# Delta-rule attention with experts on one core: state updates as full 128-row products, and exponentials written in place

## The chip, the cores and the metric

One Trainium2 chip; the program runs on one of its cores. The metric is the device time of one execution in microseconds. TensorE makes the matrix products and transposes, VectorE, ScalarE and GpSimd (POOL in the profile) the elementwise work, SyncE (SP) issues most of the DMAs. SBUF is the on-chip memory of 128 partitions, PSUM the banks that TensorE writes to.

## The reference

A layer on x of 2 batches x 2048 tokens x 256. Attention has 16 heads of 128, in segments of 64 tokens, and carries a state per batch and head from segment to segment:

```python
def step(carry, seg):                       # one segment of 64 tokens
    mem, z = carry                          # [b, h, 128, 128], [b, h, 128, 1]
    qq, kk, vv = seg
    sigma_q = jax.nn.elu(qq) + 1.0
    att_dot = softmax(causal(qq @ kk.T / scale)) @ vv
    att_mem = sigma_q @ mem / (sigma_q @ z)
    sigma_k = jax.nn.elu(kk) + 1.0
    delta = vv - sigma_k @ mem / (sigma_k @ z)
    mem_new = mem + sigma_k.T @ delta
    z_new = z + sigma_k.sum(rows)
    att = beta * att_mem + (1.0 - beta) * att_dot
    ...
x = x + attention(layernorm(x))
x = x + experts(layernorm(x))               # router, 32 experts, a shared one
```

The feature map elu(a) + 1 is max(a, 0) + min(exp(a), 1).

## The kernel before

Two functions run one after the other: `attention` and `experts`. The change is in the first.

`attention` goes through 16 blocks (`NBLK`) of 128 tokens, that is two segments for each of the two batches, and in every block through 8 groups (`NG`) of two heads (`HG`): 128 groups, counted by `n`. The state of all heads stays in SBUF in `mem`, 129 columns per head and batch (`ZC`: 128 of `mem` and one of z). Each engine has its own hand-ordered queue; semaphores join them, and every engine executes strictly in its written order.

In one group TensorE does, in this order (`body` of the tensor block, L997 to L1046): the numerators of segment 0 (`numerators`, L883: features times state, for keys into PSUM bank `chain_k` and for queries into `chain_q`); after a wait for `ksig_ready`, the key projection of the next group (`project_t`, L838, 12 products of 128x128 by 256 columns); the transposes of the group before (L927); the state update of segment 0 (`update`, L899); the query projection of the next group; in group 6 the transposes of the next block's input; in group 0 half of the output projection (`project_out`, L945); the numerators of segment 1; the transposes of the probabilities (L936); the value projection (`project_v`, L850); in groups 3, 4 and 7 some small work for the block before (`x1_transposes`, `logits`, `pick_transposes`); the key transposes of the next group (`key_transposes`, L873); the update of segment 1; the products of probabilities and values (`attend`, L910, in the 64x64 form); and the scores of the next group (`scores`, L860).

An update computes the transposed key features times `dl`, in which partitions 0 to 63 hold the 64 tokens of batch 0 and partitions 64 to 127 those of batch 1. It makes four products, for each of two heads one of batch 0 into `chain_k` (rows 0 to 63 of the array) and one of batch 1 into `chain_q` (rows 64 to 127), each with 129 moving columns. The stationary operand is `ksig`, the transposed key features. A product on f32 operands is two matmul instructions in the trace, each with its weight load; a transpose is one. The form in the profile, as 64*128 or 128*128, is the part of the array that an instruction uses.

The features come about in four steps per group: ScalarE copies the projection (`qraw`, `kraw`) and writes its exponential to `ex_q` and `ex_k` (`queries` L385, `keys` L392); GpSimd caps it at 1 in place (`cap_queries` L305, `cap_keys` L311); VectorE adds the larger of the projection and 0 and writes `sigq` and `sigk` (`sigma_q` L564, `sigma_k` L572), which have two buffers, by the parity of the group. TensorE transposes `sigk` into `bank_k`, and ScalarE copies that to `ksig` (`key_rows`, L408), once the update of segment 1 of the group before has read the old `ksig`.

VectorE makes `dl` (`delta`, L579), subtracts the update from the state (`state`, L597; `mem_ready` lets the next numerators go), and does the softmax sums, the layer norms and the router's choice of experts. ScalarE also reads out the memory's answer (`read_out`, L415) and copies values (`values`, L401); `attend` waits for the latter.

Of the kernel before, what the change touches and what calls it, by code (L numbers as in the profile page):

```python
# [19 lines left out]
HG = 2  # L20
# [45 lines left out]
def attention(nc, ctx, io, scratch):  # L66
# [31 lines left out]
    kraw = sb("kraw", [128, HG, 2, B, SEG])  # L98
    ex_q = sb("ex_q", [128, HG * 2 * B * SEG])
    ex_k = sb("ex_k", [128, HG * 2 * B * SEG])  # L100
    val = sb("val", [128, 2, HG, DK])
    vb = sb("vb", [128, 2, HG, DK])
    vo = sb("vo", [128, 2, HG, DK])
    ksig = sb("ksig", [128, HG, 2, DK])
    sm = sb("sm", [128, T, SEG])
# [172 lines left out]
    def _(pool):  # L278
# [17 lines left out]
        for half in range(2):  # L296
# [6 lines left out]
                       allow_small_or_imprecise_dtypes=True).then_inc(s["desc_ready"], 1)  # L303

        def cap_queries(n):  # L305
            pool.wait_ge(s["q_exp"], n + 1)
            stand_alone(pool, s["pool_noted"])
            nc.gpsimd.tensor_scalar(ex_q[:, :], ex_q[:, :], 1.0, None, ALU.min  # L308
                                    ).then_inc(s["q_min"], 1)

        def cap_keys(n):  # L311
            pool.wait_ge(s["k_exp"], n + 1)
            stand_alone(pool, s["pool_noted"])
            nc.gpsimd.tensor_scalar(ex_k[:, :], ex_k[:, :], 1.0, None, ALU.min  # L314
                                    ).then_inc(s["k_min"], 1)
# [52 lines left out]
    def _(act):  # L368
# [16 lines left out]
        def queries(n, first_ever=False):  # L385
            act.wait_ge(s["q_mm"], n + 1)
            nc.scalar.activation(flat(qraw), bank_q[:, :], ACT.Copy).then_inc(s["q_raw"], 1)  # L387
            if not first_ever:
                act.wait_ge(s["q_sig"], n)
            nc.scalar.activation(ex_q[:, :], bank_q[:, :], ACT.Exp).then_inc(s["q_exp"], 1)  # L390

        def keys(n, first_ever=False):  # L392
            act.wait_ge(s["k_mm"], n + 1)
            if not first_ever:
                act.wait_ge(s["s_mm"], n)
            nc.scalar.activation(flat(kraw), bank_k[:, :], ACT.Copy).then_inc(s["k_raw"], 1)
            if not first_ever:
                act.wait_ge(s["k_sig"], n)
            nc.scalar.activation(ex_k[:, :], bank_k[:, :], ACT.Exp).then_inc(s["k_exp"], 1)  # L399

# [7 lines left out]
        def key_rows(n, first_ever=False):  # L408
            act.wait_ge(s["kt_mm"], n + 1)
            if not first_ever:  # L410
                act.wait_ge(s["upd_mm"], 2 * n)
            nc.scalar.activation(ksig[:, :, :, :].rearrange("p j s d -> p (j s d)"), bank_k[:, :],  # L412
                                 ACT.Copy).then_inc(s["ksig_ready"], 1)

# [33 lines left out]
        queries(0, True)  # L448
        values(0, True)
        key_rows(0, True)  # L450

# [52 lines left out]
    def _(dve):  # L504
# [59 lines left out]
        def sigma_q(n, par):  # L564
# [3 lines left out]
                out=sigq[:, par, :, :, :, :].rearrange("p j s b t -> p (j s b t)"),  # L568
                in0=bank_q[:, :], scalar=0.0, in1=ex_q[:, :], op0=ALU.max, op1=ALU.add
                ).then_inc(s["q_sig"], 1)  # L570

        def sigma_k(n, par):  # L572
            dve.wait_ge(s["k_min"], n + 1)
            nc.vector.scalar_tensor_tensor(
                out=sigk[:, par, :, :, :, :].rearrange("p j s b t -> p (j s b t)"),
                in0=bank_k[:, :], scalar=0.0, in1=ex_k[:, :], op0=ALU.max, op1=ALU.add
                ).then_inc(s["k_sig"], 1)
# [150 lines left out]
        for seg in range(2):  # L728
            nc.vector.memset(dl[seg][:, :, DK:ZC], -1.0)
        nc.vector.memset(gsx[:, :, :], SENT)  # L730
        nc.vector.memset(glist[:, :, :], SENT)
# [95 lines left out]
    def _(pe):  # L827
# [71 lines left out]
        def update(n, seg):  # L899
# [3 lines left out]
            for j in range(HG):  # L903
                for b in range(B):
                    ins = mm((chain_k, chain_q)[b][:, j * ZC:(j + 1) * ZC],  # L905
                             ksig[ROWS[b], j, seg, :], dl[seg][ROWS[b], j, :],
                             start=True, stop=True)
# [754 lines left out]
```

## Time and profile before

| | |
|---|---|
| median of 3 runs | 1832.46 us (1832.45 to 1833.88) |
| the profiled execution, its own time | 1832.18 us |
| its span, first to last instruction | 1830.4 us |
| mean granted TensorE clock | 0.985 |
| TensorE busy: matmul | 1732.8 us, 95% of the span |
| TensorE busy: weight load, beside it | 1475.5 us, 81% |
| VectorE busy | 1206.7 us, 66% |
| ScalarE busy | 803.0 us, 44% |
| GpSimd busy | 913.0 us, 50% |
| update products (L905), 2 x 1024 instructions | 297 ns mean of one |
| key-row copies (L412), 128 | 598 ns mean of one |

How to read it: a matmul's duration in the profile runs to the modelled end of its result, so neighbours overlap; what an instruction costs in a dense stretch is the distance from its start to the next one's. The engine on which nearly no idle time is left sets the time, and a wait of another engine costs nothing by itself. Names such as bank_k<-ident,sigk give what is written and what is read; xN is the number of instructions merged in a row.

### The profile page before, as it was taken

What the parts mean: (1) busy time and instruction counts of PE and PEld (TensorE: products, weight loads), DVE (VectorE), ACT (ScalarE), POOL (GpSimd) and SP (SyncE); (2) the same over time, 40 slices, a digit from 0 to 9 for tenths busy, and PEclk for the clock granted to TensorE, in tenths of its full rate; (3) what the DMA queues carried; (4) which work ended last, traced back from release to release, by engine and by line L of the source; (5) the groups of instructions that cost most, each with busy time, mean ns of one, the idle gap of its engine ahead of it and who ended that gap; (6) DMA issues with size and microseconds to landing.
All of it is one profiled execution on the core that took longest, in us unless ns stands there. A gap on an engine that the chain in (4) does not pass through costs nothing. (4 is left out here: it accounts for less than half of the span.)

```text
span 1830.4 us, 45891 instructions
## 1 busy us (share of the span) xinstructions
PE 1732.8 (95%) x17990; PEld 1475.5 (81%) x17990; DVE 1206.7 (66%) x3996; ACT 803.0 (44%) x1934; POOL 913.0 (50%) x826
## 2 busy tenths in 40 slices
PE   6999999999999999999999999999999999984988
PEld 5788888888888888888888888888888888862545
DVE  6756757576767667575767676675757675756544
ACT  3544545353535455453535354554535353521131
POOL 4655646454646555464546465554645464620261
PEclk9999999999999999999999999999999999997999
DMA  4200000001000000000010000000000100006956
GB/s 152 81 10 25 15 19 15 25 8 32 8 14 25 15 25 15 19 15 25 7 32 7 15 25 15 25 15 20 17 22 8 32 8 9 25 14 203 273 136 196
DMA packets 83431, 75.24 MB, mean 41 GB/s; under 512 B 20992, under 2 KB 74128, under 8 KB 82960
## 3 DMA queue, kind: packets, MB, share of 16 engines
q1 hardware_dynamic: 78992, 65.96, 11.9%
q0 software_dynamic: 3376, 5.55, 1.5%
q8 instruction: 144, 2.36, 0.6%
q10 hardware_dynamic: 848, 0.79, 0.2%
q14 instruction: 71, 0.58, 0.1%
HBM read 47.78 MB, written 24.47 MB: 39 GB/s over the span
## 5 line engine op out<-in xcount | busy, mean ns | idle before, releaser
L323 POOL TENSOR_TENSOR vb<-val,beta_rows 128x512 f32<-128x512 f32 x128 | 169.3, 1322 | 243.8 <-ACT val L405 243.8
L419 ACT ACTIVATE am<-chain_q,rdq 128x128 f32<-128x128 f32 x512 | 159.3, 365 | 274.2 <-DVE rdq L585 274.0
L601 DVE TENSOR_TENSOR mem<-mem,chain_k 128x258 f32<-128x258 f32 x256 | 107.7, 421 | 252.0 <-PE chain_q L905 252.0
L348 POOL TENSOR_TENSOR sm<-sm,smx 128x256 f32<-128x256 f32 x128 | 78.5, 613 | 313.7 <-DVE smx L757 313.7
L951 PE MATMUL bank_o<-wo,att 128*128 128x256 f32 x1024 | 228.1, 381 | 0.9 <-ACT att L433 0.9
L951 PEld LDWEIGHTS bank_o<-wo,att 128*128 128x128 f32 x1024 | 193.6, 191 | 26.7 <-issue 1.3
L314 POOL TENSOR_SCALAR ex_k<-ex_k 128x512 f32<-128x512 f32 x128 | 191.0, 1492 | 43.9 <-ACT ex_k L399 43.9
L308 POOL TENSOR_SCALAR ex_q<-ex_q 128x512 f32<-128x512 f32 x128 | 190.1, 1485 | 0.3 <-POOL vo L332 0.3
L895 PE MATMUL chain_k<-mem,sigk 128*64 128x129 f32 x2048 | 165.5, 281 | 20.9 <-DVE mem L601 20.9
L905 PE MATMUL chain_k<-dl,ksig 64*128 64x129 f32 x1024 | 181.4, 297 | 2.2 <-ACT am L419 1.6
L905 PE MATMUL chain_q<-dl,ksig 64*128 64x129 f32 x1024 | 181.6, 297 | 0.0
L905 PEld LDWEIGHTS chain_k<-dl,ksig 64*128 64x128 f32 x1024 | 132.4, 186 | 45.3 <-issue 42.3
L332 POOL TENSOR_TENSOR vo<-val,vb 128x512 f32<-128x512 f32 x128 | 164.3, 1284 | 0.0
L591 DVE SCALAR_TENSOR_TENSOR dl<-chain_k,rdk,vb 128x128 f32<-128x128 f32 x512 | 154.6, 343 | 6.2 <-DVE rdk L582 0.8
L895 PE MATMUL chain_q<-mem,sigq 128*64 128x129 f32 x2048 | 157.7, 273 | 0.0
L355 POOL TENSOR_TENSOR pd<-sm,sinv 128x256 f32<-128x256 f32 x128 | 78.4, 612 | 153.0 <-DVE sinv L765 153.0
L412 ACT ACTIVATE ksig<-bank_k 128x512 f32<-128x512 f32 x128 | 76.6, 598 | 160.3 <-PE chain_q L905 155.6
L895 PEld LDWEIGHTS chain_k<-mem,sigk 128*64 128x64 f32 x2048 | 108.9, 137 | 43.9 <-issue 29.8
L387 ACT ACTIVATE qraw<-bank_q 128x512 f32<-128x512 f32 x128 | 76.4, 597 | 135.2 <-PE bank_q L846 135.2
L905 PEld LDWEIGHTS chain_q<-dl,ksig 64*128 64x128 f32 x1024 | 132.5, 186 | 0.0
L895 PEld LDWEIGHTS chain_q<-mem,sigq 128*64 128x64 f32 x2048 | 122.3, 136 | 0.0
L846 PE MATMUL bank_k<-xt_hi,w_hi 128*128 128x256 f32 x512 | 117.1, 311 | 1.1 <-DVE xt_lo L559 1.1
(193 smaller groups left out, 4337.1 us busy)
## 6 DMA issues: line engine op xcount, KB each, us to landing
w<-in_L_ffn_w_dram SPq DMA_DIRECT2D x16, 512.0 KB, 8.1
expert_rows<-w_in SPq DMA_DIRECT2D x16, 288.0 KB, 2.2
expert_sums<-zero SPq DMA_DIRECT2D x16, 272.0 KB, 5.0
x_in<-in_L_attn_x_dram SPq DMA_DIRECT2D x16, 256.0 KB, 3.0
x_res<-in_L_attn_x_dram SPq DMA_DIRECT2D x16, 256.0 KB, 3.2
x_rows<-w_in SPq DMA_DIRECT2D x16, 256.0 KB, 2.0
x_normed_t<-x1t SPq DMA_DIRECT2D x16, 256.0 KB, 2.1
xt_all<-x_normed_t SPq DMA_DIRECT2D x4, 1024.0 KB, 13.3
```

What stands on the lines that cost most here:

```text
L308: nc.gpsimd.tensor_scalar(ex_q[:, :], ex_q[:, :], 1.0, None, ALU.min).then_inc(s["q_min"], 1)
L314: nc.gpsimd.tensor_scalar(ex_k[:, :], ex_k[:, :], 1.0, None, ALU.min).then_inc(s["k_min"], 1)
L323: nc.gpsimd.tensor_tensor(vb[:, :, :, :].rearrange("p s j d -> p s (j d)"), val[:, :, :, :].rearrange("p s j d -> p s (j d)"), rows.unsque ...
L332: nc.gpsimd.tensor_tensor(vo[:, :, :, :], val[:, :, :, :], vb[:, :, :, :], ALU.subtract).then_inc(s["vo_ready"], 1)
L348: nc.gpsimd.tensor_tensor(sm[:, :, :], sm[:, :, :], smx[:, :].unsqueeze(2).to_broadcast([128, T, SEG]), ALU.subtract).then_inc(s["s_shifte ...
L419: ins = nc.scalar.activation(am[:, par, seg, j, :], chain_q[:, j * ZC:j * ZC + DK], ACT.Copy, scale=rdq[:, seg, j:j + 1])
L591: ins = nc.vector.scalar_tensor_tensor(out=dl[seg][:, j, 0:DK], in0=chain_k[:, j * ZC:j * ZC + DK], scalar=rdk[:, seg, j:j + 1], in1=vb[:, ...
L601: ins = nc.vector.tensor_tensor(m, m, (chain_k, chain_q)[b][:, 0:HG * ZC].rearrange("p (j z) -> p j z", j=HG), ALU.subtract)
L846: ins = mm(out, w[:, g, m, c, col], x[:, c, :, :].rearrange("p s t -> p (s t)"), start=i == 0, stop=i == len(parts) - 1)
L895: ins = mm(out[ROWS[half], j * ZC:(j + 1) * ZC], sig[:, j, seg, b, :], mem[:, HG * g + j, b, :], start=True, stop=True)
L905: ins = mm((chain_k, chain_q)[b][:, j * ZC:(j + 1) * ZC], ksig[ROWS[b], j, seg, :], dl[seg][ROWS[b], j, :], start=True, stop=True)
L951: ins = mm(bank_o[:, b * D:(b + 1) * D], att[:, b * PIECES + i, :], wo[:, i, :], start=(i == 0 and b == 0), stop=(i == PIECES - 1), skip_g ...
```

## The change

- The copy of the transposed key features goes to `ksig` with one more dimension, the batch. Batch 0's 64 rows go to its own part of the buffer, batch 1's to another, and the other batch's rows of each part are zero, written once at the start by a memset on VectorE. The copy is so two instructions of 64 partitions instead of one of 128.
- The four products of an update take all 128 rows of `ksig` and of `dl`. The zero rows add nothing, so the results are the same.
- The exponentials are written to `sigq` and `sigk` themselves, capped there and turned into the features there; `ex_q` and `ex_k` go, and with them ScalarE's waits for `q_sig` and `k_sig`.
- ScalarE waits for `zero_ready` once before the first copy of key rows.

```diff
--- before.py
+++ after.py
@@ -96,12 +96,11 @@
     sigk = sb("sigk", [128, 2, HG, 2, B, SEG])
     qraw = sb("qraw", [128, HG, 2, B, SEG])
     kraw = sb("kraw", [128, HG, 2, B, SEG])
-    ex_q = sb("ex_q", [128, HG * 2 * B * SEG])
-    ex_k = sb("ex_k", [128, HG * 2 * B * SEG])
     val = sb("val", [128, 2, HG, DK])
     vb = sb("vb", [128, 2, HG, DK])
     vo = sb("vo", [128, 2, HG, DK])
-    ksig = sb("ksig", [128, HG, 2, DK])
+
+    ksig = sb("ksig", [128, HG, 2, B, DK])
     sm = sb("sm", [128, T, SEG])
     pd = sb("pd", [128, T, SEG])
     smx = sb("smx", [128, T])
@@ -302,16 +301,20 @@
         nc.gpsimd.iota(desc[:, :, :], pattern=[[-S, B], [-1, BLK]], base=N, channel_multiplier=0,
                        allow_small_or_imprecise_dtypes=True).then_inc(s["desc_ready"], 1)
 
+        def flat(t, n):
+
+            return t[:, n % 2, :, :, :, :].rearrange("p j s b t -> p (j s b t)")
+
         def cap_queries(n):
             pool.wait_ge(s["q_exp"], n + 1)
             stand_alone(pool, s["pool_noted"])
-            nc.gpsimd.tensor_scalar(ex_q[:, :], ex_q[:, :], 1.0, None, ALU.min
+            nc.gpsimd.tensor_scalar(flat(sigq, n), flat(sigq, n), 1.0, None, ALU.min
                                     ).then_inc(s["q_min"], 1)
 
         def cap_keys(n):
             pool.wait_ge(s["k_exp"], n + 1)
             stand_alone(pool, s["pool_noted"])
-            nc.gpsimd.tensor_scalar(ex_k[:, :], ex_k[:, :], 1.0, None, ALU.min
+            nc.gpsimd.tensor_scalar(flat(sigk, n), flat(sigk, n), 1.0, None, ALU.min
                                     ).then_inc(s["k_min"], 1)
 
         def values_kept(n, g, first_ever=False):
@@ -385,18 +388,14 @@
         def queries(n, first_ever=False):
             act.wait_ge(s["q_mm"], n + 1)
             nc.scalar.activation(flat(qraw), bank_q[:, :], ACT.Copy).then_inc(s["q_raw"], 1)
-            if not first_ever:
-                act.wait_ge(s["q_sig"], n)
-            nc.scalar.activation(ex_q[:, :], bank_q[:, :], ACT.Exp).then_inc(s["q_exp"], 1)
+            nc.scalar.activation(flat(sigq[:, n % 2]), bank_q[:, :], ACT.Exp).then_inc(s["q_exp"], 1)
 
         def keys(n, first_ever=False):
             act.wait_ge(s["k_mm"], n + 1)
             if not first_ever:
                 act.wait_ge(s["s_mm"], n)
             nc.scalar.activation(flat(kraw), bank_k[:, :], ACT.Copy).then_inc(s["k_raw"], 1)
-            if not first_ever:
-                act.wait_ge(s["k_sig"], n)
-            nc.scalar.activation(ex_k[:, :], bank_k[:, :], ACT.Exp).then_inc(s["k_exp"], 1)
+            nc.scalar.activation(flat(sigk[:, n % 2]), bank_k[:, :], ACT.Exp).then_inc(s["k_exp"], 1)
 
         def values(n, first_ever=False):
             act.wait_ge(s["v_mm"], n + 1)
@@ -409,8 +408,11 @@
             act.wait_ge(s["kt_mm"], n + 1)
             if not first_ever:
                 act.wait_ge(s["upd_mm"], 2 * n)
-            nc.scalar.activation(ksig[:, :, :, :].rearrange("p j s d -> p (j s d)"), bank_k[:, :],
-                                 ACT.Copy).then_inc(s["ksig_ready"], 1)
+            for b in range(B):
+                ins = nc.scalar.activation(
+                    ksig[ROWS[b], :, :, b, :].rearrange("p j s d -> p (j s) d"),
+                    bank_k[ROWS[b], :].rearrange("p (c d) -> p c d", d=DK), ACT.Copy)
+            ins.then_inc(s["ksig_ready"], 1)
 
         def read_out(n, par, seg):
 
@@ -447,6 +449,7 @@
         keys(0, True)
         queries(0, True)
         values(0, True)
+        act.wait_ge(s["zero_ready"], 2)
         key_rows(0, True)
 
         def body(blk, first, last):
@@ -566,14 +569,14 @@
             dve.wait_ge(s["q_min"], n + 1)
             nc.vector.scalar_tensor_tensor(
                 out=sigq[:, par, :, :, :, :].rearrange("p j s b t -> p (j s b t)"),
-                in0=bank_q[:, :], scalar=0.0, in1=ex_q[:, :], op0=ALU.max, op1=ALU.add
+                in0=bank_q[:, :], scalar=0.0, in1=sigq[:, par, :, :, :, :].rearrange("p j s b t -> p (j s b t)"), op0=ALU.max, op1=ALU.add
                 ).then_inc(s["q_sig"], 1)
 
         def sigma_k(n, par):
             dve.wait_ge(s["k_min"], n + 1)
             nc.vector.scalar_tensor_tensor(
                 out=sigk[:, par, :, :, :, :].rearrange("p j s b t -> p (j s b t)"),
-                in0=bank_k[:, :], scalar=0.0, in1=ex_k[:, :], op0=ALU.max, op1=ALU.add
+                in0=bank_k[:, :], scalar=0.0, in1=sigk[:, par, :, :, :, :].rearrange("p j s b t -> p (j s b t)"), op0=ALU.max, op1=ALU.add
                 ).then_inc(s["k_sig"], 1)
 
         def delta(n, seg):
@@ -727,6 +730,7 @@
         nc.vector.memset(mem[:, :, :, DK:ZC], 1.0 / DK)
         for seg in range(2):
             nc.vector.memset(dl[seg][:, :, DK:ZC], -1.0)
+        nc.vector.memset(ksig[:, :, :, :, :], 0.0)
         nc.vector.memset(gsx[:, :, :], SENT)
         nc.vector.memset(glist[:, :, :], SENT)
         nc.vector.memset(tmpx[:, :, :], SENT)
@@ -903,7 +907,7 @@
             for j in range(HG):
                 for b in range(B):
                     ins = mm((chain_k, chain_q)[b][:, j * ZC:(j + 1) * ZC],
-                             ksig[ROWS[b], j, seg, :], dl[seg][ROWS[b], j, :],
+                             ksig[:, j, seg, b, :], dl[seg][:, j, :],
                              start=True, stop=True)
             ins.then_inc(s["upd_mm"], 1)
```

## Rows read from the trace of the kernel before

**Rows 1.** the page's part 2, granted clock of TensorE in 40 slices, in tenths

```profile
PEclk9999999999999999999999999999999999997999
```

**Rows 2.** busy us (x instructions) of each engine in one steady block

```profile
320.96:421.53 100.57, 98.91 (x1091) 86.95 (x1091) 69.37 (x237) 47.44 (x115) 53.58 (x48) 1.00 0.06 18
```

**Rows 3.** waits of TensorE in ten steady blocks: total us, times, longest

```profile
PE chain_k L895 <- DVE mem L601: 10.8, 10, 1.1
PE bank_a L922 <- ACT val L405: 5.9, 20, 0.3
```

**Rows 4.** the same view, first block

```profile
PE bank_a L922 <- ACT val L405: 3.8, 6, 1.1
PE chain_k L895 <- DVE mem L601: 3.6, 6, 0.7
```

**Rows 5.** timeline of TensorE around update 0: start us, us, instructions

```profile
1004.26 0.40 PE L846 MATMUL bank_k<-xt_hi,w_lo 128*128 128x256 f32 x2
1004.50 0.60 PE L932 MATMUL bank_a<-by_piece,am 128*128 128x128 f32 x4
1005.03 0.37 PE L905 MATMUL chain_k<-dl,ksig 64*128 64x129 f32 x1
1005.03 0.37 PE L905 MATMUL chain_q<-dl,ksig 64*128 64x129 f32 x1
1005.24 0.27 PE L905 MATMUL chain_k<-dl,ksig 64*128 64x129 f32 x1
...
1005.36 0.27 PE L905 MATMUL chain_k<-dl,ksig 64*128 64x129 f32 x1
...
1005.67 0.51 PE L846 MATMUL bank_q<-xt_hi,w_hi 128*128 128x256 f32 x2
1006.02 0.40 PE L846 MATMUL bank_q<-xt_lo,w_hi 128*128 128x256 f32 x2
```

**Rows 6.** the same view, transposes that follow one another

```profile
977.33 0.60 PE L961 MATMUL bank_o<-ident,w_in 128*128 128x128 f32 x4
977.76 0.60 PE L878 MATMUL bank_k<-ident,sigk 128*128 128x128 f32 x4
```

**Rows 7.** the same view, output projection, and router products

```profile
1030.20 7.07 PE L951 MATMUL bank_o<-wo,att 128*128 128x256 f32 x32
1037.20 0.66 PE L895 MATMUL chain_k<-mem,sigk 128*64 128x129 f32 x8
...
988.50 0.97 PE L969 MATMUL bank_o<-gwt,x1t 128*128 128x32 f32 x8
989.31 0.63 PE L878 MATMUL bank_k<-ident,sigk 128*128 128x128 f32 x4
```

**Rows 8.** timeline of all engines around update 1

```profile
999.70 0.60 PE L878 MATMUL bank_k<-ident,sigk 128*128 128x128 f32 x4
...
1000.87 0.33 PE L922 MATMUL bank_a<-vo,pt 64*64 64x128 f32 x2
...
1001.05 0.60 ACT L412 ACTIVATE ksig<-bank_k 128x512 f32<-128x512 f32 x1 [0.56 <-PE chain_q L905]
...
1001.33 0.42 DVE L601 TENSOR_TENSOR mem<-mem,chain_q 128x258 f32<-128x258 f32 x1
...
1001.47 0.69 PE L869 MATMUL bank_s<-kraw,qraw 128*64 128x64 f32 x16
...
1001.98 0.61 PE L895 MATMUL chain_k<-mem,sigk 128*64 128x129 f32 x8
...
1002.97 0.51 PE L846 MATMUL bank_k<-xt_hi,w_hi 128*128 128x256 f32 x2
```

**Rows 9.** ScalarE by lines, a steady block: busy us, mean ns, idle before

```profile
L390 ACT ACTIVATE ex_q<-bank_q 128x512 f32<-128x512 f32 x8 | 4.7, 592 | 0.0
```

**Rows 10.** timeline of VectorE at the start

```profile
12.35 3.47 DVE L726 MEMSET mem<- 128x4096 f32 x1 [0.80 <-issue]
...
18.65 1.76 DVE L507 TENSOR_TENSOR w_lo<-w_in,w_hi 128x1536 fp32r<-128x1536 f32 x1 [2.62 <-ACT w_hi L374]
```

## The prediction

> **What bounds the kernel now.** I read the page's clock row first, then the busy times by stretch, then the waits of TensorE alone, and last the timeline of single product groups. The granted clock is nine tenths or more in 39 of the 40 slices [rows 1] and 1.00, the level of 2.4 GHz, in a steady block [rows 2], so between the two versions only instructions and waits can differ. The attention part, 128 groups of two heads in 16 blocks of 8, fills most of the span: a steady block takes 100.57 us, and 16 of them would be 1609 us of 1830. In it TensorE is busy 98.91 us, VectorE 69.37, ScalarE 47.44, GpSimd 53.58 [rows 2]. TensorE sets the pace, and its waits are few and regular: over ten blocks it waits 10 times for the state update on VectorE, 1.08 us each (after group 7 of a block), and 20 times for the copy of the values on ScalarE, 0.295 us each (groups 3 and 6) [rows 3]. The first block has more of both, 3.6 and 3.8 us over six or seven groups [rows 4]. So what one group's products cost on TensorE counts 128 times, save where one of these waits takes it up.
>
> **Part 1, the products.** Each update has four source products, each two instructions in the trace. Before, the product of batch 0 uses array rows 0 to 63 and that of batch 1 rows 64 to 127, and the rows show them as pairs: both start within 0.01 us, and the next pair 0.11 to 0.12 us later [rows 5]. So eight instructions take four steps. After, all eight use the full array and can only follow one another: eight steps.
>
> What this mode costs at its edges is to be seen too. The four transposes ahead of update 0 start at 1004.50 and the update at 1005.03, 0.53 us. Four transposes followed by others of the same kind take 0.43 us (977.33 to 977.76) [rows 6], so the switch into 64-row mode costs 0.10 us of drain. Its first pair is followed by the second only after 0.21 us (1005.03 to 1005.24), 0.10 more than a step: a weight load with nothing to hide it. From the last pair to the next work it is 0.20 us. Then the projection's first two products take 0.35 us (1005.67 to 1006.02), where two take 0.24 us elsewhere (1004.26 to 1004.50): again an uncovered load. Update 0 stands between two stretches of 128-row work, so after the change both switches go. Update 1 comes after 128-row transposes but ahead of 64x64 products, so only the switch into it goes.
>
> How fast a full-array f32 product with 129 moving columns repeats, no row shows. The nearest rows: 256 columns take 0.219 us each (32 in 7.00 us, 1030.20 to 1037.20, the last drain in it), so their weight load is hidden and half the columns would stream in 0.108 us; with 32 moving columns, where only the load of 128 columns can count, 8 take 0.81 us, 0.101 each (988.50 to 989.31) [rows 7]; the projections repeat at 0.119 us, with loads of the same size [rows 5]. I take 0.112 us: the stream of 129 columns (0.108, as in the pairs) and a few ns for the load, near the first row. The bounds are 0.101 and 0.119.
>
> Update 0, from the first transpose ahead of it to the third product of the projection: before 1006.02 - 1004.50 = 1.52 us. After 4 x 0.108 + 8 x 0.112 + 0.24 = 1.57 us. That is +0.05 us.
> Update 1, from the first key transpose to the first 64x64 product: before 1000.87 - 999.70 = 1.17 us [rows 8]. After 4 x 0.108 + 7 x 0.112 + 0.20 = 1.42 us. That is +0.25 us.
> Together +0.30 us a group; 128 groups make +38 us if no wait takes any of it.
>
> The Trainium skill speaks against this change more strongly: "TensorEngine Tiling (Array Packing)", section "Theoretical Speedup", gives up to a factor of two for a dimension of 64 or less. As a factor on the steps alone this would be 4 x 0.11 = 0.44 us more per update, 0.88 per group, +113 us in all, and a time of 1945. The trace has that factor on the steps but takes most of it back at the edges, which that section leaves out; I go by the rows.
>
> **What the waits take up.** In groups 3 and 6 TensorE waits 0.295 us for the values' copy, which ScalarE makes after another copy that itself follows work of TensorE ahead of update 1. The chain is released before update 1 and does not lengthen with it, so the 0.25 us of update 1 go into this wait. After group 7 the 1.08 us wait is for VectorE's chain of gate weights, picks, query features and state, released from the group's softmax early in the group; it takes both updates, 0.30 us. A steady block so grows by 8 x 0.30 - 2 x 0.25 - 0.30 = 1.6 us; 15 blocks 24 us. In the first block the waits of rows 4 (over 0.5 us each) take up update 1 in nearly every group, leaving 8 x 0.05 = 0.4 us. Sum +24.4 us.
>
> **Part 2, the key rows' copy.** One 128x512 copy of 0.60 us becomes two of 64 partitions with 512 elements each. No row shows the shorter form. Bounds: half each if partitions counted (nothing added), 0.60 each back to back (+0.60 us); I take the upper end less the 0.1 us by which neighbours overlap, since a copy's time goes with the elements per partition, +0.5 us per group. What is late next: the projection of keys waits for it. In the group shown the copy ends at 1001.65 and the projection starts at 1002.97, 1.32 us later, and TensorE shows no wait there [rows 8]. The +0.5 fits, and behind it on ScalarE only the memory read-out is queued, which needs the numerators that end after 1002.97. Cost nothing; without that cover, up to 0.5 x 128 = 64 us.
>
> **Part 3, exponentials in place.** Exponentials, caps and maxima keep count and size. Two waits of ScalarE go; the exponential of the queries already started with no idle time in front, 0.592 us each [rows 9], so nothing is gained. Cost nothing.
>
> **Part 4, the start.** The zeroing of the key-row buffer is a 128x1024 memset on VectorE. The 128x4096 one took 3.47 us, so about 0.87 us, in front of a 2.62 us idle time [rows 10]; ScalarE's new wait for it stands ahead of a copy that begins at 23.8 us, long after, and queues nothing. Cost nothing; uncovered, 0.9 us once.
>
> **The rivals.**
> *Weight loads are not hidden (slower by much).* If every full-array product paid load and stream, 0.21 us as the first after a switch does [rows 5]: update 0 is 4 x 0.108 + 8 x 0.21 + 0.24 - 1.52 = +0.83, update 1 0.43 + 7 x 0.21 + 0.20 - 1.17 = +0.93; 1.76 x 128 = 225 us, less the waits of 15 x 1.67 + 7.4 = 32: about +193, 2025 us. Against it: the 256-column products and the projections both hide a load of the same size [rows 5, 7]. Chance 0.03. The skill's "TensorE: Matmul & The Clock Gate", section "The mechanism" of its part on packing, says that weight loads overlap a running product only when the row group differs; that rule would give this case. The rows with full-array products disagree with it.
> *The waits move instead of shrinking (slower).* If the chains of ScalarE and VectorE start later with the update, nothing is taken up: +38, 1871 us. It could be so if they are not released where I read it. Chance 0.08.
> *The state update comes too late (slower).* Numerators start 1001.98, the state's last addition ends 1001.75 [rows 8]; the signal takes part of the 0.23 us. If the deeper products end 0.05 us later than the margin allows, 100 groups lose 5 us: 1862. It decides from about 0.1 us. Chance 0.05, inside the range.
> *The switches pay for the steps (faster).* Break-even: with a step of s us update 0 differs by 8s - 0.85 and update 1 by 7s - 0.54; a steady block has the first 7 times and the second 5 times uncovered, and their sum is zero at s = 0.095. Below it the kernel is faster. The densest products with small moving tiles, the scores, make 16 instructions in 0.51 us, 0.064 per pair [rows 8]; at that step updates differ by -0.34 and -0.09 us, times 128 about -55 us, 1778. Against it: nothing on the full array repeats in under 0.101 us, even with 32 columns [rows 7]. Chance 0.04. At the bound 0.101 itself a block grows by 0.6 us, +8 us, 1841: still slower.
> *The change does less than it says.* The longer step could be hidden wholly by waits: they amount to 1.67 us a block and stand in three groups of eight, so five groups must show it. Within 0.2%, by the same sum, only for a step of 0.092 to 0.098 us: chance 0.03.
> *The copies come late.* If two copies took over 1.9 us together (1.32 us slack): 0.02, from 0.3 us late about +38 more, 1895.
>
> **The numbers.** The profiled execution took 1832.18 us, the median of the runs 1832.46; +24.4 on the latter gives 1856.9. The likeliest case (step 0.108 to 0.119, waits taking up their part) has chance 0.75: at 0.108 a block grows by 1.2 us, 1850.5; at 0.119 by 2.2 us, 1866. The range 1844 to 1871 adds the late state update, half of the way to the 0.101 bound and the waits that move. About 0.2% (3.7 us) is what a measurement of this kernel can tell from no change. Faster 0.04, same 0.03, slower 0.93.
>
> **What would show it.** The timeline of the update: eight instructions of 128*128 form at 0.112 us steps, transposes ahead at 0.108 with no drain. Steady blocks of 102.2 us instead of 100.57. The value waits shrink from 0.295 to 0.05 us or go, the state wait from 1.08 to about 0.78. Key-row copies: two, 1.1 us from the first's start to the second's end, and TensorE without a wait ahead of the key projection. VectorE and GpSimd unchanged in busy time. Wrong would be a step outside 0.101 to 0.119, a new wait of TensorE for the key rows, or a wait for the state in every group.

## The result, and the profile after

The changed kernel takes 1857.93 us in the median, the kernel before 1832.64 us beside it: 1.0136 times as long, with a 95% interval of 1.0119 to 1.0153. The growth is 25.3 us; the forecast was 1857 us, 24.4 us more. One of the changed kernel's four executions took 6463.26 us at a mean granted clock of 0.418 and stays out of the ratio; the median of the other three is 1857.78 us, 25.1 us more. The profiled execution took 1858.08 us with a span of 1856.3 us.

The page of the changed kernel, its first part (busy us, share of the span, instructions):

```profile
PE 1772.1 (95%) x17990; PEld 1571.5 (85%) x17990; DVE 1218.3 (66%) x3997; ACT 876.8 (47%) x2062; POOL 917.5 (49%) x826
```

TensorE is busy 39 us longer than before, ScalarE 74 us (the second copy of the key rows), VectorE 12 us, GpSimd 5 us. Only TensorE is near its span.

One steady block, in the same view as [rows 2]:

```profile
325.24:427.46 102.22, 101.30 (x1090) 92.91 (x1091) 70.11 (x237) 52.02 (x123) 53.83 (x48) 1.00 0.06 18
```

The block takes 102.22 us where it took 100.57; the forecast was 102.2. The granted clock is 1.00 as before.

TensorE's waits in ten steady blocks (total us, times, longest), against [rows 3]:

```profile
PE chain_k L899 <- DVE mem L604: 8.3, 10, 0.8
```

The 20 waits for the value copies are gone from the view; what is left of them in the trace is 0.05 us each. The wait for the state after group 7 is 0.83 us instead of 1.08.

The timeline of TensorE around update 0, against [rows 5]; a row of L909 with x2 holds the two instructions of one product:

```profile
965.73 0.60 PE L936 MATMUL bank_a<-by_piece,am 128*128 128x128 f32 x4
966.17 0.39 PE L909 MATMUL chain_k<-dl,ksig 128*128 128x129 f32 x2
966.39 0.39 PE L909 MATMUL chain_q<-dl,ksig 128*128 128x129 f32 x2
966.62 0.39 PE L909 MATMUL chain_k<-dl,ksig 128*128 128x129 f32 x2
966.84 0.39 PE L909 MATMUL chain_q<-dl,ksig 128*128 128x129 f32 x2
966.98 0.48 PE L850 MATMUL bank_q<-xt_hi,w_hi 128*128 128x256 f32 x2
967.30 0.40 PE L850 MATMUL bank_q<-xt_lo,w_hi 128*128 128x256 f32 x2
```

Eight instructions of the update follow one another, two every 0.22 to 0.23 us; the last starts at 966.95 and the first of the projection at 966.98. From the first transpose to the third projection product it is 967.30 - 965.73 = 1.57 us (1.52 before). The four transposes now take 0.44 us, with no drain behind them, where they took 0.53.

The same view around update 1, against [rows 8]:

```profile
960.69 0.60 PE L882 MATMUL bank_k<-ident,sigk 128*128 128x128 f32 x4
961.13 0.39 PE L909 MATMUL chain_k<-dl,ksig 128*128 128x129 f32 x2
...
961.80 0.39 PE L909 MATMUL chain_q<-dl,ksig 128*128 128x129 f32 x2
962.12 0.33 PE L926 MATMUL bank_a<-vo,pt 64*64 64x128 f32 x2
```

962.12 - 960.69 = 1.43 us (1.17 before): eight steps take the place of four and only the entry is saved.

The costliest groups of the page that the change touches (busy us, mean ns | idle before, releaser):

```profile
L412 ACT ACTIVATE ksig<-bank_k 64x512 f32<-64x512 f32 x256 | 151.5, 592 | 192.1 <-PE chain_q L909 187.5
...
L909 PE MATMUL chain_k<-dl,ksig 128*128 128x129 f32 x1024 | 199.7, 276 | 2.4 <-ACT am L421 1.7
L909 PE MATMUL chain_q<-dl,ksig 128*128 128x129 f32 x1024 | 198.0, 275 | 0.0
```

### The profile page after: what moved, and what is told of

Read it like the earlier page. It is cut to its first block and busy times, and to the rows that moved or that the text cites. A ratio compares the mean times of both kernels' runs of the same rounds, so it can differ in the third digit from the quotient of the medians.

```text
span 1856.3 us, 46021 instructions
## 1 busy us (share of the span) xinstructions
PE 1772.1 (95%) x17990; PEld 1571.5 (85%) x17990; DVE 1218.3 (66%) x3997; ACT 876.8 (47%) x2062; POOL 917.5 (49%) x826
## 5 line engine op out<-in xcount | busy, mean ns | idle before, releaser
L604 DVE TENSOR_TENSOR mem<-mem,chain_k 128x258 f32<-128x258 f32 x256 | 107.9, 421 | 288.3 <-PE chain_q L909 287.2
L412 ACT ACTIVATE ksig<-bank_k 64x512 f32<-64x512 f32 x256 | 151.5, 592 | 192.1 <-PE chain_q L909 187.5
L317 POOL TENSOR_SCALAR sigk<-sigk 128x512 f32<-128x512 f32 x128 | 193.9, 1515 | 44.5 <-ACT sigk L398 44.5
L909 PE MATMUL chain_k<-dl,ksig 128*128 128x129 f32 x1024 | 199.7, 276 | 2.4 <-ACT am L421 1.7
L909 PE MATMUL chain_q<-dl,ksig 128*128 128x129 f32 x1024 | 198.0, 275 | 0.0
L311 POOL TENSOR_SCALAR sigq<-sigq 128x512 f32<-128x512 f32 x128 | 190.1, 1485 | 2.0 <-POOL vo L335 0.3
L899 PE MATMUL chain_k<-mem,sigk 128*64 128x129 f32 x2048 | 165.6, 281 | 17.2 <-DVE mem L604 17.2
L335 POOL TENSOR_TENSOR vo<-val,vb 128x512 f32<-128x512 f32 x128 | 164.1, 1282 | 0.0
L909 PEld LDWEIGHTS chain_k<-dl,ksig 128*128 128x128 f32 x1024 | 155.0, 191 | 4.9 <-DVE dl L594 3.2
L909 PEld LDWEIGHTS chain_q<-dl,ksig 128*128 128x128 f32 x1024 | 154.8, 191 | 0.0
L472 ACT ACTIVATE pt<-bank_s 128x256 f32<-128x256 f32 x128 | 49.3, 385 | 153.0 <-PE bank_s L944 153.0
```

The costliest lines, as they stand in the source:

```text
L311: nc.gpsimd.tensor_scalar(flat(sigq, n), flat(sigq, n), 1.0, None, ALU.min).then_inc(s["q_min"], 1)
L317: nc.gpsimd.tensor_scalar(flat(sigk, n), flat(sigk, n), 1.0, None, ALU.min).then_inc(s["k_min"], 1)
L335: nc.gpsimd.tensor_tensor(vo[:, :, :, :], val[:, :, :, :], vb[:, :, :, :], ALU.subtract).then_inc(s["vo_ready"], 1)
L412: ins = nc.scalar.activation(ksig[ROWS[b], :, :, b, :].rearrange("p j s d -> p (j s) d"), bank_k[ROWS[b], :].rearrange("p (c d) -> p c d", ...
L604: ins = nc.vector.tensor_tensor(m, m, (chain_k, chain_q)[b][:, 0:HG * ZC].rearrange("p (j z) -> p j z", j=HG), ALU.subtract)
L899: ins = mm(out[ROWS[half], j * ZC:(j + 1) * ZC], sig[:, j, seg, b, :], mem[:, HG * g + j, b, :], start=True, stop=True)
```

## Where the growth lies, group by group

The length of a group is taken from its first numerator product to that of the next group, worked out from the traces as the mean of 13 steady blocks. In these terms the changed kernel stands against the one before:

```
us            g0     g1     g2     g3     g4     g5     g6     g7    block
before      24.20  10.33  10.38  11.16  11.18  10.35  11.16  11.81  100.56
changed     24.50  10.62  10.63  11.17  11.48  10.78  11.24  11.85  102.26
difference   0.30   0.29   0.25   0.02   0.29   0.43   0.09   0.04    1.70
forecast     0.30   0.30   0.30   0.05   0.30   0.30   0.05   0.00    1.60
```

15 blocks of 1.70 us are 25.5 us, and the first block grew by 0.15 us. The stretch ahead of the first group changed by +0.6 us, that from the last group on by -0.3. So the growth is in the attention part, and its pattern is the forecast's, with one cell out of line: group 5.

## The experiments

Theory: TensorE sets the time; a full-array product repeats at 0.112 us, the mode switches that go give part back, and three waits a block take up part of the rest. The rivals: the second copy or the in-place exponentials carry part of it; the updates cost equal halves; the waits only move; the step is set by something else than the forecast took.

### Exponentials in place, alone

One of its two lines, against the kernel before:

```diff
-            nc.scalar.activation(ex_q[:, :], bank_q[:, :], ACT.Exp)
+            nc.scalar.activation(flat(sigq[:, n % 2]), bank_q[:, :], ACT.Exp)
```

> Only the exponentials in place; key rows copied in one piece and updates in the 64-row form, as before. Theory (serial products on TensorE make the whole growth): 1832.6 us, within 0.1% of before. Rival (the in-place writing or the two dropped waits of ScalarE shift work on ScalarE, VectorE and GpSimd so that TensorE waits more or less): a change of over 2 us either way.

Measured 1832.85 us against 1832.88 of before, ratio 0.9999 (0.9989 to 1.0008). A steady block is 100.54 us. This part of the change is free and brings nothing.

### Two key-row copies, with the updates in the 64-row form

```diff
-                             ksig[:, j, seg, b, :], dl[seg][:, j, :],
+                             ksig[ROWS[b], j, seg, b, :], dl[seg][ROWS[b], j, :],
```

> The changed kernel with the updates back in the 64-row form: two key-row copies of 64 partitions, the zeroed buffer and the exponentials in place stay. Theory: the copies fit into their slack of 1.32 us, so 1832.6 us, within 0.1% of before. Rival (the second copy carries part of the growth): 1835 to 1858 us, with a wait of TensorE ahead of the key projection.

Measured 1832.79 us, ratio 1.0000 (0.9991 to 1.0010). TensorE's waits in ten steady blocks are those of [rows 3]:

```profile
PE chain_k L899 <- DVE mem L604: 10.8, 10, 1.1
PE bank_a L926 <- ACT val L404: 6.0, 20, 0.4
```

None is for the key rows. The second copy, the zeroing and the new wait at the start cost nothing; all 25 us come from the form of the products.

### One update at a time

```diff
+                    rows = slice(0, BLK) if seg == 0 else ROWS[b]
                     ins = mm((chain_k, chain_q)[b][:, j * ZC:(j + 1) * ZC],
-                             ksig[:, j, seg, b, :], dl[seg][:, j, :],
+                             ksig[rows, j, seg, b, :], dl[seg][rows, j, :],
```

These are the lines for update 0 alone; for update 1 alone the test is `seg == 1`.

> The changed kernel with only update 0 in the 128-row form, update 1 in 64-row form. Theory (serial steps of 0.112 us, both switches around update 0 gone, +0.05 us in each group that no wait covers): 1832.6 + 7 x 15 x 0.05 + 0.4 = 1838.3 us. Rival (a product costs the same in both updates, so each carries half): 1845 us.

> The changed kernel with only update 1 in the 128-row form, update 0 in 64-row form. Theory (+0.25 us in the five groups of a block that no wait covers, nothing in the first block): 1832.6 + 5 x 15 x 0.25 = 1851.1 us. Rival (equal halves): 1845 us. Rival (waits move and take nothing up): 1832.6 + 128 x 0.25 = 1864.6 us.

Update 1 alone: 1850.10 us, ratio 1.0088 (1.0071 to 1.0105), 17.2 us more where 18.5 were expected. Groups 0, 1, 2, 4 and 5 grew by 0.27, 0.24, 0.21, 0.25 and 0.24 us, groups 3, 6 and 7 by -0.02, -0.02 and 0.00 us. The waits of ten blocks:

```profile
PE chain_k L899 <- DVE mem L604: 8.3, 10, 0.8
```

The value waits are out of the view and the state wait is 0.83 us. So the waits take up update 1 fully, and "the waits move" (1864.6 us) falls.

Update 0 alone: 1844.48 us, ratio 1.0058 (1.0041 to 1.0074). Expected were 1838.3; it is 11.6 us more than before and not 5.7. Seven groups grew by 0.04 to 0.09 us, close to the forecast, but group 5 by 0.44 us. Its waits in ten blocks:

```profile
PE chain_k L899 <- DVE mem L604: 13.1, 20, 1.1
PE bank_a L927 <- ACT val L404: 5.6, 19, 0.3
```

20 waits for the state instead of 10: a second one per block, ahead of group 6, 0.23 us each. This was not expected, and equal halves (1845 us) would have fitted the total by chance; the groups show that it is one group and one wait.

The wait costs more than the 0.23 us of the view. TensorE's scores in such a group 5 and the next numerators:

```profile
1008.89 0.69 PE L873 MATMUL bank_s<-kraw,qraw 128*64 128x64 f32 x16
1009.80 0.66 PE L899 MATMUL chain_k<-mem,sigk 128*64 128x129 f32 x8 [0.23 <-DVE mem L604]
```

From start to start it is 0.91 us, and 0.52 us in the groups without this wait. The view counts idle time from the modelled end of the scores, and in a dense stretch the numerators start 0.17 us ahead of that end. So a wait of 0.23 us here costs 0.40.

### Why group 5: an addition that misses its gap

In group 5 VectorE makes the router's scores after the first state update of the group. The kernel before, VectorE (state's last part, then the bias addition L643) and GpSimd (caps L314, values' multiplication L332), start us, us:

```profile
995.79 0.42 DVE L601 TENSOR_TENSOR mem<-mem,chain_q 128x258 f32<-128x258 f32 x1
...
996.93 0.22 DVE L643 TENSOR_TENSOR w_in<-w_in,gbias 128x64 f32<-128x64 f32 x1
```

```profile
995.63 1.49 POOL L314 TENSOR_SCALAR ex_k<-ex_k 128x512 f32<-128x512 f32 x1 [0.26 <-ACT ex_k L399]
997.09 1.28 POOL L332 TENSOR_TENSOR vo<-val,vb 128x512 f32<-128x512 f32 x1
```

The changed kernel, the same instructions (L604, L646; L317, L335):

```profile
1011.50 0.42 DVE L604 TENSOR_TENSOR mem<-mem,chain_q 128x258 f32<-128x258 f32 x1
...
1012.65 1.27 DVE L646 TENSOR_TENSOR w_in<-w_in,gbias 128x64 f32<-128x64 f32 x1
```

```profile
1011.11 1.49 POOL L317 TENSOR_SCALAR sigk<-sigk 128x512 f32<-128x512 f32 x1 [0.26 <-ACT sigk L398]
1012.56 1.27 POOL L335 TENSOR_TENSOR vo<-val,vb 128x512 f32<-128x512 f32 x1
```

Before, the addition starts at 996.93, 0.16 us ahead of GpSimd's multiplication, and takes 0.22 us. After, it starts at 1012.65, 0.09 us behind the multiplication's start, and takes 1.27 us: it ends at 1013.92, just behind the multiplication (1013.83). What stands behind it on VectorE comes late, the second delta and the second state update among it. With update 0 alone TensorE meets this as the wait for the state. In the changed kernel it meets it in update 1, which takes that delta: from the key transposes to the first 64x64 product it is 1.56 us in group 5 and 1.42 us with the addition moved, as in the run below. What moved it is update 0. Its stretch is only 0.05 us longer, but its last instruction starts 1.22 us after the first transpose (966.95) where before it was 0.98 us (1005.48, the last instruction of the update, in the stretch of [rows 5]), 0.24 us later, since the steps stand before the result and the saved switch stands partly behind it. GpSimd's cap starts as long after that transpose as before (1.48 and 1.47 us), so VectorE alone has moved.

The Trainium skill has this contention on its page "SBUF — State Buffer", section "Who interferes with whom": a VectorE instruction with two SBUF inputs and a GpSimd one that reads SBUF exclude each other, and the first keeps the ports to its end. The pair of addition and multiplication agrees, 0.22 against 1.27 us. The trace of before has a case that does not: its addition runs its 0.22 us while GpSimd's cap of 1.49 us, which also reads SBUF, is under way (995.63 to 997.12; the profile's spans of GpSimd are rough). So has the run below: its addition runs from 1003.07 to 1003.40 inside a cap from 1002.71 to 1004.20.

To test it, the addition goes behind the second delta of the group, where GpSimd makes a cap:

```diff
         def gate_scores(blk):
...
-            link(v.tensor_tensor(scb[:, :, :], score[:, :, :], gbias[:, :, :], ALU.add), True)
         def gate_group_sums(blk):
-            link, v = gate_link(blk, 3), nc.vector
+            link, v = gate_link(blk, 2), nc.vector
+            link(v.tensor_tensor(scb[:, :, :], score[:, :, :], gbias[:, :, :], ALU.add), True)
...
```

> As the run with only update 0 in the 128-row form, but the router's bias addition on VectorE in group 5 is made after the second delta of the group instead of before the key features. Theory (in that run and in the changed kernel the addition came just after GpSimd had begun its values' multiplication, waited 1.0 us for it, and made group 5 up to 0.4 us longer): the addition takes 0.22 us again, group 5 grows by 0.05 instead of 0.44 us, and the time is 1844.5 - 15 x 0.39 = 1838.6 us. Rival (the late state update in group 5 has another cause): 1844.5 us.

Measured 1839.85 us, ratio 1.0043 (1.0026 to 1.0060). The additions in VectorE's groups by line:

```profile
L650 DVE TENSOR_TENSOR w_in<-w_in,gbias 128x64 f32<-128x64 f32 x16 | 5.1, 319 | 0.0
```

0.32 us instead of 1.21 (0.22 were expected), and group 5 is 10.39 us where it was 10.79: +0.04 on before, as the other groups. The state waits are 10 again. The median is 4.6 us under that of the run with the addition in its old place, where 5.9 were expected, and the rival (1844.5 us) falls. The profiled execution alone, 1834.96 us, would mislead: its steady block is 0.36 us longer than before, as the theory wants, but its last part happens to be 3.9 us shorter.

The same move in the whole changed kernel:

> The whole changed kernel with the router's bias addition of group 5 moved behind the second delta. Theory (the blocked addition delays the second delta and costs TensorE 0.14 us in group 5 of each block, besides the 0.30 us of the products): group 5 of a steady block falls from 10.78 to 10.64 us in the trace, about 2 us in all, 1856 us, which one execution can hardly tell; the group's length decides. Rival (the 0.14 us come from the products themselves): group 5 stays at 10.78 us.

```profile
L650 DVE TENSOR_TENSOR w_in<-w_in,gbias 128x64 f32<-128x64 f32 x16 | 5.1, 318 | 0.0
```

Group 5 falls from 10.78 to 10.62 us, and the block from 102.26 to 102.11. This was one execution, 1855.24 us, and its total decides nothing; the group's length does: the 0.16 us are the blocked addition's.

### What sets the step

```diff
-                    ins = mm((chain_k, chain_q)[b][:, j * ZC:(j + 1) * ZC],
-                             ksig[:, j, seg, b, :], dl[seg][:, j, :],
+                    ins = mm((chain_k, chain_q)[b][:, j * ZC + 64:(j + 1) * ZC],
+                             ksig[:, j, seg, b, :], dl[seg][:, j, 64:ZC],
```

> The changed kernel, but the update products move only 65 of the 129 columns (the last 64 of a head's state and its z); the rest of the state is left out, so the output is not the reference's. It tells what sets the step of 0.112 us of a full-array product. Theory (the load of 128 stationary columns): the step stays at 0.11 us, 1858 us. Rival (the stream of the moving columns): the step falls to 0.06 us and the time to about 1775 us.

Measured 1860.36 us, ratio 1.0151 (1.0134 to 1.0168), with a steady block of 102.21 us against 102.26. The timeline of TensorE in update 0, two instructions in a row:

```profile
966.11 0.33 PE L909 MATMUL chain_k<-dl,ksig 128*128 128x65 f32 x2
966.28 0.39 PE L909 MATMUL chain_q<-dl,ksig 128*128 128x65 f32 x2
966.50 0.39 PE L909 MATMUL chain_k<-dl,ksig 128*128 128x65 f32 x2
966.73 0.39 PE L909 MATMUL chain_q<-dl,ksig 128*128 128x65 f32 x2
```

Half the moving columns, and still 0.22 to 0.23 us for two; only the very first instruction is followed sooner, after 0.06 us. So the stream of the moving columns doesn't set the step. What all these products have in common is the load of 128 stationary columns, and with 64 stationary and 64 moving columns, in the scores, an instruction follows every 0.032 us (16 in 0.51 us [rows 8]). That makes the load the likely cause; no run changes it alone, and transposes, with a load of the same size, repeat at 0.108 us.

The trace of before already had this step. The eight router products with 32 moving columns [rows 7] start at 988.50, 988.53, 988.64, 988.76 and then every 0.11 us up to 989.20: from the second on the step is 0.112 us. The 0.101 us of the prediction is the mean over eight with the short first one in it, and no lower bound for the step. The forecast had the right number but gave it mostly to the stream.

### Longer and shorter updates, in the kernel before

Each product of update 1 twice:

```diff
             for j in range(HG):
-                for b in range(B):
+                for _ in range(1 + seg):
+                    for b in range(B):
```

> The kernel before, with each product of update 1 issued twice in the 64-row form (the second overwrites the first with the same values): four more steps of 0.11 us, 0.44 us a group. Theory (the chains behind the value copies and behind the long VectorE work of group 7 don't move with update 1, so the waits of 0.295 us in groups 3 and 6 and of 1.08 us after group 7 take up what fits): 5 x 0.44 + 2 x (0.44 - 0.295) = 2.5 us a steady block, nothing in the first block, so 1832.8 + 37 = 1870 us. Rival (nothing is taken up): 1832.8 + 128 x 0.44 = 1889 us.

Measured 1866.23 us, ratio 1.0189 (1.0172 to 1.0206), 33.7 us more. Groups 0, 1, 2, 4 and 5 grew by 0.41 to 0.45 us; groups 3 and 6 by 0.08, group 7 by nothing. The state wait of ten blocks:

```profile
PE chain_k L895 <- DVE mem L601: 6.3, 10, 0.6
```

It has fallen from 1.08 to 0.63 us, by the 0.45 of the update. That "nothing is taken up" (1889 us) falls. Groups 3 and 6 took up 0.36 us and not the 0.295 of the wait. This is again how the view counts: a pair of the update lasts 0.27 us there, and the product behind it starts 0.20 us after the pair's start when it waits for nothing (as in [rows 5]). So this wait costs 0.07 us more than it shows, 0.365 us.

Update 1 in quarters of the array, the other way:

```diff
-                for b in range(B):
-                    ins = mm((chain_k, chain_q)[b][:, j * ZC:(j + 1) * ZC],
-                             ksig[ROWS[b], j, seg, :], dl[seg][ROWS[b], j, :],
+                for h in range(1 + seg):
+                    half, cols = (ROWS[h], slice(h * 64, h * 64 + 64)) if seg else (...)
+                    for b in range(B):
+                        ins = mm((chain_k, chain_q)[b][half, j * ZC:(j + 1) * ZC],
+                                 ksig[ROWS[b], j, seg, cols], dl[seg][ROWS[b], j, :],
```

> The kernel before, with update 1 in the 64x64 form, each product in two halves of 64 stationary columns, so that four products run at once and the products of probabilities and values behind it need no switch. Theory (a switch costs about 0.09 us of drain and, with 64-column loads, 0.05 us of uncovered load; four steps stay four steps): 0.14 us less a group on TensorE, taken back by longer waits in groups 3, 6 and 7, and 0.05 us of it by the state update, which has only 0.09 us to spare: 1826 us, between 1822 and 1830. Rival (the 16 instructions are too many for four steps): slower than before by up to 0.4 us a group, 1865 us.

Measured 1828.43 us, ratio 0.9978 (0.9968 to 0.9987): 4.1 us less than before, a little less than expected but in its bounds. TensorE's timeline from the key transposes to the next numerators:

```profile
955.05 0.60 PE L878 MATMUL bank_k<-ident,sigk 128*128 128x128 f32 x4
955.58 0.32 PE L907 MATMUL chain_k<-dl,ksig 64*64 64x129 f32 x1
...
955.97 0.27 PE L907 MATMUL chain_k<-dl,ksig 64*64 64x129 f32 x1
...
956.10 0.33 PE L924 MATMUL bank_a<-vo,pt 64*64 64x128 f32 x2
...
956.70 0.69 PE L869 MATMUL bank_s<-kraw,qraw 128*64 128x64 f32 x16
957.35 0.33 PE L895 MATMUL chain_k<-mem,sigk 128*64 128x129 f32 x2
```

Sixteen instructions make four steps, and from the last of them to the next products it is 0.12 us instead of 0.20. From 955.05 to 956.70 it is 1.65 us, where the same stretch of before takes 1.77 (999.70 to 1001.47) [rows 8]. But the scores to the numerators now take 0.65 us where before took 0.51, in the group shown: the state update lets only part of the gain through. Over all groups, 0, 2, 4 and 5 became 0.05 to 0.13 us shorter and 1, 3 and 6 0.02 to 0.06 us longer.

### Without the waits

If waits take up 0.8 us of a block's growth, taking their causes away should bring it out. In the kernel before and in the changed one alike, VectorE's descriptor step leaves group 7, and ScalarE copies the values first:

```diff
+                if g == 4 and blk >= 2:
+                    next_desc(blk)
...
+                if nxt:
+                    values(n + 1)
                 if g == 3 and not first:
                     side_x1t(blk)
...
                 if g == NG - 2 and not last:
-                    act.wait_ge(s["v_mm"], n + 2)
                     xt_hi_part(blk + 2)
                 if nxt:
-                    values(n + 1)
                     key_rows(n + 1)
```

> The kernel before with the causes of TensorE's steady waits moved: VectorE's step of the descriptor (0.98 us in group 7) goes to group 4, and ScalarE copies the values ahead of the transposed rows in group 3 and of the new input in group 6. The products are unchanged. Theory (these causes make the waits of 1.08 and twice 0.295 us): 0.98 + 0.59 = 1.57 us less a steady block, 1832.5 - 15 x 1.57 = 1809 us. Rival (other work of the two engines takes their place): 1820 to 1832 us.

> The changed kernel with the same moves. Theory (the waits took up 0.80 us a block of what the longer updates cost, and with the waits gone nothing does): the run without waits in the 64-row form + 128 x 0.30, that is 1809 + 38 = 1847 us, or up to 3 us more if VectorE's addition in group 5 still waits for GpSimd. Rival (the waits took up nothing, and the updates just cost 25 us): 1809 + 25 = 1834 us.

> Update 1 in the 64x64 form, as in the run of that form, with the same moves. Theory (0.14 us less a group on TensorE, of which the state update leaves 0.09 us, now in all groups): the run without waits in the 64-row form - 128 x 0.09, that is 1809 - 11 = 1798 us. Rival (the state update is the next bound and lets nothing of it through): 1809 us.

The kernel before with the moves: 1812.07 us, ratio 0.9891 (0.9875 to 0.9906). It is 3 us off the 1809. One wait stayed, for the state after group 7:

```profile
PE chain_k L900 <- DVE mem L601: 2.9, 10, 0.3
```

The changed kernel with the moves: 1841.32 us, ratio 1.0052 (1.0038 to 1.0066), and no wait of TensorE is left in the view of that stretch. Group lengths of the two:

```
us                    g0     g1     g2     g3     g4     g5     g6     g7    block
before, moved       24.19  10.33  10.38  10.78  11.18  10.35  10.85  11.06   99.13
changed, moved      24.50  10.62  10.63  11.06  11.50  10.77  11.11  10.96  101.14
difference           0.31   0.29   0.25   0.28   0.32   0.42   0.26  -0.10    2.01
```

Between these two the change costs 29.3 us, not 25.3. By the total alone that would be nearer to the rival's 25 than to the theory's 38. The groups decide: 3 and 6, which hid it before, now show 0.28 and 0.26 us like the others, which the rival doesn't allow. Group 7 grew by 0.04 us and now shrinks by 0.10: before its change the moved kernel still had the wait of 0.285 us, which by the count above costs 0.45 us, and from the scores to the next numerators it is 0.97 us there and 0.63 us after it. The theory's 38 us took that wait for gone. That is 15 x 0.40 = 6.0 us of the 9 us by which the theory is off; the first block, which grew by 0.26 us and not by 8 x 0.30, is another 2.1.

The quarters with the moves: 1806.92 us, ratio 0.9859 (0.9843 to 0.9874). That is 5.2 us below the moved kernel before, not the 11 expected; groups 0, 2, 3 and 5 are 0.09 to 0.13 us shorter, but 1, 4 and 6 are 0.01 to 0.06 us longer, and in group 7 the state wait grew from 0.285 to 0.49 us and takes all of it. It is the fastest version here, 1.4% under the kernel before and 2.7% under the changed one.

## Why the prediction was right, step by step

*TensorE sets the pace.* Right: the copies and the in-place part measured as nothing, and every added step of TensorE counted where no wait stood.

*The step of 0.112 us.* Right in size, 0.22 to 0.23 us for two in the trace. Its cause was wrong: it is not the stream, as the run with 65 columns shows. The bound of 0.101 us came from a mean over eight starts. The rival without hidden loads (0.21 us) is out: the loads run beside the products.

*Update 0, +0.05 us.* Right for the stretch on TensorE, 1.52 to 1.57. Two of its terms were off by as much in opposite directions: the eight steps read 0.81 us from 966.17 to 966.98 where the sum has 0.90, and the two projection products behind them 0.32 us where it has 0.24. What the step left out is when its result comes: 0.24 us later. Two things hang on that. Group 5 costs 0.16 us more than its products, 2.4 us in all. And group 7 did not take up update 0's part: the state wait fell by 0.25 us to 0.83, and the forecast had 0.78. In the traces the first state update of group 7 starts 0.23 us later after the group's start, and VectorE's last one 0.04 us later (0.06 with update 0 alone); the traces don't show why that much and no more.

*Update 1, +0.25 us.* Right, 1.17 to 1.43.

*The waits.* Right for groups 3 and 6, where 0.295 us went down to 0.05, and nearly for group 7. Each costs 0.07 (values) or 0.17 us (state) more than the view shows, which the sum didn't need as long as a rest of the wait stayed. The runs with a single update, with update 1 twice and without the waits show that they give once what they have.

*The first block.* 0.15 us more where 0.4 was forecast. Between the kernels of this document the first block differs by up to 2.3 us (94.5 to 96.8), so the traces can't tell the two.

*The copies.* Right that they cost nothing. The sum had them overlap by 0.1 us; they do not. The ScalarE copy and then TensorE's key projection in one group of the changed kernel:

```profile
972.89 1.19 ACT L412 ACTIVATE ksig<-bank_k 64x512 f32<-64x512 f32 x2 [0.79 <-PE chain_q L909]
```

```profile
974.82 0.50 PE L850 MATMUL bank_k<-xt_hi,w_hi 128*128 128x256 f32 x2
```

Two copies of 64 partitions take 1.19 us, 0.592 us each by the page, as long as one of 128 partitions did, and end at 974.08. The projection starts at 974.82, so 0.74 us of the 1.32 us of slack are left.

*VectorE and GpSimd unchanged in busy time.* Wrong: VectorE 12 us more. The blocked additions alone are 15.7 us (3.6 to 19.3 us over 16 of them); others changed both ways, the largest a `gm` operation of 16 that fell from 18.2 to 9.8 us and a copy to `glist` that rose from 2.7 to 7.6 us. What moved those no run tests.

The errors of the terms nearly cancel. In a steady block groups 0 to 4 are together 0.10 us under their forecast and groups 5 to 7 0.21 us over it; the first block is 0.25 us under. So the 0.9 us between forecast and growth is smaller than some of its parts' errors.

## What to carry to other kernels

On an engine that is never idle, ask of a packed form what it saves in steps and what its entries and exits cost: here pairs of 64-row products save 0.45 us per update, and the switches give back 0.40 us where both go, 0.20 us where one goes. Cost the time at which the result comes apart from the length of the stretch; the length decides what the engine does next, the time of the result what the others do. And before adding work to the busiest engine, or taking it away, look where it waits: a wait gives or takes what fits into it, and only the rest is seen. The idle time that a view shows can be less than what the wait costs, so compare start to start with a place where nothing is waited for.

## What the runs showed of the hardware that was not expected

- Four 64x64 tiles at once hold the step of 0.11 us even as 16 instructions with 129 moving columns each, and products of the same form behind them follow with no drain.
- Full-array f32 products with 128 stationary columns repeat at 0.112 us with 32, 65 and 129 moving columns alike.
- A VectorE addition of 0.22 us took 1.27 us for having come 0.09 us after a GpSimd multiplication, and was not held by a GpSimd cap with one input (0.22 and 0.33 us).
- A ScalarE copy of 64 partitions takes 0.592 us, one with 128 took 0.598 us.
- The time from the start of the last attention group on, nearly all of it the experts' part that no edit touched, took between 209.3 and 215.6 us in the traces of these kernels. For effects of a few microseconds the lengths of the groups were the better measure than the total.
